# A vision-transformer layer on one core: the patch embedding of tiles 3 to 10 from fp16 high and low parts instead of fp32

## The reference

```
h = patches @ W.T + b                      # [32, 36, 768] x [768, 256]: the embedding
h = concat([cls_tok, h], axis=1)           # [32, 37, 256]
h = h + attention(layernorm(h))            # 4 heads, causal, with a linear memory read
h = h + moe(layernorm(h))                  # a shared FFN and the top 2 of 8 experts, hidden 1024
```

## Time and profile before

| | |
|---|---|
| median of 3 runs | 326.1 us (325.4 lowest, 1746.54 highest) |
| profiled execution | 325.89 us |
| its span | 324.0 us |
| granted TensorE clock | 0.996 |
| PE busy | 306.7 us, 95% |
| PEld busy | 259.6 us, 80% |
| DVE busy | 223.4 us, 69% |
| ACT busy | 184.5 us, 57% |
| POOL busy | 152.1 us, 47% |

### The profile page before, as it was taken

The page is one execution under the profiler, slowest core; times in us unless marked ns, Lnnn a source line. Parts: engine busy times, 40 slices in busy tenths (PEclk is TensorE's granted clock), DMA queues, the critical chain, the costliest instruction groups (busy, mean ns, idle before and its releaser), DMA issues.

```text
span 324.0 us, 9888 instructions
## 1 busy us (share of the span) xinstructions
PE 306.7 (95%) x3521; PEld 259.6 (80%) x3521; DVE 223.4 (69%) x502; ACT 184.5 (57%) x355; POOL 152.1 (47%) x208
## 2 busy tenths in 40 slices
PE   8789999999998999999999999999999999999990
PEld 6678788988777999999997777777787787777870
DVE  0637888888898989999886868755554546565530
ACT  1366768878896978476768878733232332323220
POOL 0577747777586322112622344656353544434131
PEclk9999999999999999999999999999999999999998
DMA  7775335322241117814798774243323242333121
GB/s 231 260 222 210 108 111 179 111 83 77 77 124 58 32 31 205 269 24 95 195 275 309 185 239 110 45 67 41 60 42 59 34 67 35 54 48 46 22 34 16
DMA packets 18642, 36.37 MB, mean 112 GB/s; under 512 B 3331, under 2 KB 10982, under 8 KB 18598
## 3 DMA queue, kind: packets, MB, share of 16 engines
q1 hardware_dynamic: 12166, 27.71, 26.2%
q0 software_dynamic: 6432, 8.03, 16.3%
HBM read 28.52 MB, written 7.21 MB: 110 GB/s over the span
## 4 chain that ended last, share of the span: by engine, by line
PE 76%; DVE 9%; DMA 4%; POOL 3%; issue 3%; ACT 2%; SPq 1%; POOLq 1%; DVEq 0%; ACTq 0%
PE bank L820 21%; PE bank L833 14%; PE bank L643 7%; PE bank L835 6%; PE bank L500 6%; PE bank L602 6%; DMA out_rows<-y,add_id 2%; PE bank L525 2%; PE bank L551 2%; DMA weights<-in_patches 2%; PE bank L591 2%; PE bank L565 1%; PE bank L555 1%; DVE weights L1309 1%; PE bank L453 1%
## 5 line engine op out<-in xcount | busy, mean ns | idle before, releaser
L820 PEld LDWEIGHTS bank<-x_t,weights 128*128 x1248 | 87.5, 98 | 25.5 <-issue 0.2
L820 PE MATMUL bank<-x_t,weights 128*128 128x128 f16 x1248 | 103.8, 219 | 0.0
L1002 ACT ACTIVATE act_out<-bank 128x512 f32<-128x512 f32 (+2 forms) x72 | 42.0, 585 | 86.1 <-PE bank L820 71.8
L1270 POOL DMA_INDIRECT out_rows<-y,add_id x26 | 43.0, 1653 | 69.6 <-DVE y L1626 48.1
L833 PE MATMUL bank<-weights,hid_hi 128*128 x192 | 73.3, 382 | 0.2
L1417 DVE SCALAR_TENSOR_TENSOR hid_lo<-act_out,hid_hi 128x512 f16<-128x512 f32 (+2 forms) x72 | 48.6, 680 | 12.5 <-ACT hid_hi L1013 11.0
L835 PE MATMUL bank<-weights,hid_lo 128*128 x192 | 52.3, 273 | 0.0
L1423 DVE SCALAR_TENSOR_TENSOR weights<-stage,weights 128x1024 f16<-128x1024 f32 x36 | 43.0, 1221 | 0.7 <-ACT weights L959 0.7
L959 ACT ACTIVATE weights<-stage 128x1024 f16<-128x1024 f32 x36 | 36.8, 1049 | 0.0
L1237 POOL DMA_INDIRECT slot_rows<-x_rows,gather_id x26 | 28.0, 1075 | 13.0 <-DMA out_rows<-y 5.2
L500 PE MATMUL bank<-weights 128*111 128x256 f32 x132 | 31.3, 386 | 1.6 <-DMA weights<-in_patches 1.1
(11 more groups left out here) (164 smaller groups left out, 522.8 us busy)
## 6 DMA issues: line engine op xcount, KB each, us to landing
stage<-in_w_ffn SPq DMA_DIRECT2D x36, 512.0 KB
weights<-in_patches SPq DMA_DIRECT2D x11, 333.0 KB, 3.3
x_rows<-rows SPq DMA_DIRECT2D x11, 111.0 KB
out_rows<-weights SPq DMA_DIRECT2D x10, 111.0 KB
out_rows<-y POOLq DMA_DIRECT2D x9, 119.0 KB, 5.3
weights<-in_w_embed SPq DMA_DIRECT2D x3, 256.0 KB, 4.2
stage<-in_w_qk SPq DMA_DIRECT2D x1, 512.0 KB, 6.9
slot_rows<-x_rows,gather_id POOLq DMA_INDIRECT x26, 4.1
```

The source lines that it names most:

```text
L820: mm = nc.tensor.matmul(o, weights[:, bass.ds(base + 2 * k * CHUNK + 2 * (col - col % D) + w * D + col % D, P)], x_t[:, b, (2 * x + k) * P ...
L1002: nc.scalar.activation(d_, s_, ACT.Silu, scale=1.0 / (X_SCALE * W_SCALE)).then_inc(hid_acted, 1)
L1270: nc.gpsimd.indirect_dma_start(out=out, out_offset=bass.IndirectOffsetOnAxis(ap=add_id[:, j:j + 1], axis=0), in_=y[:, y_place(j)], in_offs ...
```

## The change

- The embeddings of tiles 3 to 10 take three products of fp16 parts (low patches by high weights, high by low, high by high, in that order), so 18 fp16 matmuls for 6 fp32 ones. Tiles 0 to 2 stay as they are.
- The embedding's weights are split once, at the start: the high part is the first thing on ScalarE's queue (128x1024, then 128x512), the low part stands on VectorE between `embed_h(0)` and `embed_h(1)`.
- Each of tiles 3 to 10 has its patches (128x666) split. The high part is put at the end of ScalarE's step: tiles 3, 4, 5 and 6 in steps 0 to 3, and tiles 7 to 10 in steps 3 to 6 (two of them in step 3). The low part is put on VectorE behind `embed_h` in steps 0 to 2 (tiles 3 to 5), and from step 3 on between `split_lo` and `embed_h(s+2)` (tile `s+3`, to step 7).
- `embed_h` of these tiles scales and adds in one instruction, and the patches' buffer is free once the low part is written, not once the embedding is done.

```diff
+F16_FROM = 3
+P_SCALE = 16.0
+EMBED_PRODUCTS = ((1, 0), (0, 1), (0, 0))
...
             def load_patches(t):
-                if t >= PATCH_RING:
-                    sp.wait_ge(embed_ready, t - PATCH_RING + 1)
+                held = t - PATCH_RING
+                if held >= F16_FROM:
+                    sp.wait_ge(patch_lo, held - F16_FROM + 1)
+                elif held >= 0:
+                    sp.wait_ge(embed_ready, held + 1)
...
             def embed(t):
-                pe.wait_ge(patches_in[t % PATCH_RING], 16 * (t // PATCH_RING + 1))
+                if t < F16_FROM:
+                    pe.wait_ge(patches_in[t % PATCH_RING], 16 * (t // PATCH_RING + 1))
+                else:
+                    pe.wait_ge(patch_lo, t - F16_FROM + 1)
+                if t == F16_FROM:
+                    pe.wait_ge(we_lo, 2)
...
+                if t >= F16_FROM:
+                    for n, (x, w) in enumerate(EMBED_PRODUCTS):
+                        for k in range(PC):
+                            we = we_front[:, k, w] if k < 4 else we_back[:, k - 4, w]
+                            mm = nc.tensor.matmul(embed_bank(t), patch_pair[t % 2][:, x, k * T:(k + 1) * T], we,
+                                                  start=(n == 0 and k == 0), stop=(n == 2 and k == PC - 1))
+                    mm.then_inc(embed_ready, 1)
+                    return
...
+            def split_patches_hi(t):
+                act.wait_ge(patches_in[t % PATCH_RING], 16 * (t // PATCH_RING + 1))
+                if t >= F16_FROM + 2:
+                    act.wait_ge(embed_ready, t - 1)
+                nc.scalar.mul(patch_pair[t % 2][:, 0], s_patch[:, t % PATCH_RING].rearrange("p a b -> p (a b)"),
+                              P_SCALE).then_inc(patch_hi, 1)
...
                 if 0 <= s - 5:
                     copy_x2_t(s - 5)
+                if s <= F16_FROM:
+                    split_patches_hi(s + 3)
+                if F16_FROM <= s < NT - 4:
+                    split_patches_hi(s + 4)
...
+            def split_patches_lo(t):
+                dve.wait_ge(patch_hi, t - F16_FROM + 1)
+                nc.vector.scalar_tensor_tensor(
+                    out=patch_pair[t % 2][:, 1], in0=s_patch[:, t % PATCH_RING].rearrange("p a b -> p (a b)"),
+                    scalar=P_SCALE, in1=patch_pair[t % 2][:, 0], op0=ALU.mult,
+                    op1=ALU.subtract).then_inc(patch_lo, 1)
...
                 if s == 0:
                     embed_h(0)
+                    we_lo_of(0, we_front, s_we[:, 0:4])
+                    we_lo_of(1, we_back, s_we[:, 4:])
                     embed_h(1)
...
                 for c in chunks_at(s):
                     split_lo(c)
+                if F16_FROM <= s < NT - 3:
+                    split_patches_lo(s + 3)
                 if s + 2 < NT:
                     embed_h(s + 2)
+                if s < F16_FROM:
+                    split_patches_lo(s + 3)
```

More of the change, by code:

```diff
@@ L101, in build @@
         y = sb("y", [P, 3, D])
+        we_front = hid_hi.rearrange("p a b -> p (a b)").rearrange("p (k w d) -> p k w d", w=2, d=D)
+        we_back = hid_lo.rearrange("p a b -> p (a b)")[:, 0:2 * 2 * D].rearrange(
+            "p (k w d) -> p k w d", w=2, d=D)
+        patch_pair = [ap[:, 0:2 * PC * T].rearrange("p (w n) -> p w n", w=2) for ap in (
+            act_out.rearrange("p a b -> p (a b)").bitcast(F16),
+            slot_rows.rearrange("p a b -> p (a b)"))]
         space = weights[:, EARLY * EW:].bitcast(F32)
@@ L208, in build @@
         embed_ready = sem("embed_ready")
+        we_hi = sem("we_hi")
+        we_lo = sem("we_lo")
+        patch_hi = sem("patch_hi")
+        patch_lo = sem("patch_lo")
         h_ready = sem("h_ready")
@@ L1016, in shared_silu @@
                 silu_half(n, tokens_of(n), half_)
+            def split_patches_hi(t):
[4 more added lines that the diff above has]
+                              P_SCALE).then_inc(patch_hi, 1)
+            for part_ in range(EMBED_PARTS):
+                act.wait_ge(embed_in[part_], 16)
+                if part_ == 1:
+                    nc.scalar.mul(we_front[:, :, 0], s_we[:, 0:4], W_SCALE).then_inc(we_hi, 1)
+                if part_ == 2:
+                    nc.scalar.mul(we_back[:, :, 0], s_we[:, 4:], W_SCALE).then_inc(we_hi, 1)
             act.wait_ge(w_qk_in, 16)
@@ L1300, in embed_h @@
                     dve.wait_ge(rstd1, t - 1)
-                nc.vector.tensor_tensor(h[0:T, t % RING], embed_bank(t), s_eb[0:T],
-                                        ALU.add).then_inc(h_ready, 1)
+                if t < F16_FROM:
+                    nc.vector.tensor_tensor(h[0:T, t % RING], embed_bank(t), s_eb[0:T],
+                                            ALU.add).then_inc(h_ready, 1)
+                else:
+                    nc.vector.scalar_tensor_tensor(out=h[0:T, t % RING], in0=embed_bank(t),
+                                                   scalar=1.0 / (P_SCALE * W_SCALE), in1=s_eb[0:T],
+                                                   op0=ALU.mult, op1=ALU.add).then_inc(h_ready, 1)
                 dve.wait_ge(h_ready, t + 1)
@@ L1361, in proj_lo_of, with we_lo_of @@
                                                op0=ALU.mult, op1=ALU.subtract).then_inc(proj_lo, 1)
+            def we_lo_of(n, dst, src):
+                dve.wait_ge(we_hi, n + 1)
+                nc.vector.scalar_tensor_tensor(out=dst[:, :, 1], in0=src, scalar=W_SCALE, in1=dst[:, :, 0],
+                                               op0=ALU.mult, op1=ALU.subtract).then_inc(we_lo, 1)
+            def split_patches_lo(t):
[4 more added lines that the diff above has]
+                    op1=ALU.subtract).then_inc(patch_lo, 1)
             def xln_lo(t):
```

## The result

The changed kernel takes 332.93 us in the median of four executions (331.93 to 335.24), for 325.94 before: a ratio of 1.022 (95% interval 1.018 to 1.025). It is slower, by 7.0 us; 330.6 was forecast. Five more executions on another occasion gave 332.18 us and a ratio of 1.020 (1.018 to 1.022). The profiled execution took 331.93 us with a span of 329.6, 5.6 more than before.

A forecast was written before the change was run, and what follows sets the result against it. The prediction took PE as the bound, with VectorE 0.8 to 0.9 us below it. To 325.89 us it added 3.7 for the wait at tile 6 and 1.0 for GpSimd's loop: 330.6 us, range 327.6 to 333.4.

The forecast's parts named there:

- Which engines are near the bound: Steady steps of the front phase: PE full at 8.72 us, VectorE 0.8 to 0.9 us below it, idle only ahead of `embed_h`.
- The prices of the instructions: Per tile: eighteen fp16 matmuls 1.98 us for 2.77; low part 0.84 on VectorE, high part about 0.7 on ScalarE, `embed_h` sum 0.43.
- The weights' split at nothing: At the start: 1.9 us on VectorE and 1.7 on ScalarE, covered by waits, so counted as nothing; uncovered up to 1.9 us.
- The wait at tile 6: Step 3: VectorE stands 2.9 us for ScalarE's high part of tile 6; `residual(0)` comes 3.7 us late.
- GpSimd's loop: Steps 5 to 8: low parts block GpSimd up to 0.84 us, `residual` intervals become 9.3, 9.2, 9.2 us; 1.0 us in sum.
- The end: Step 8 gives back 0.3 us; the second phase, with PE 95% busy, takes up nothing of the delay.
- Rival 1: Steps 5 to 8: only the wait costs, GpSimd slips between two splits, steps of 8.9 us or less; 329.3 us, 15%.
- Rival 2: Steps 3 to 7: VectorE's five low parts each wait for a GpSimd operation, 5 x 0.5 us on top; 333 us, 9%.
- Rival 3: PE's idle before `mix_values(0)` and `scores(2)` halves its clock, costing 4 us more, part of it hidden by VectorE; 334 us, 6%.
- Rivals 4 and 5: 4: steps 9 to 12 give back 3 to 4 us, 327 us, 8%; 5: PE stays the bound, 320 us, 2%.
- The 1.5 us at tile 5: Steps 2 and 3: tile 5's low part waits for ScalarE's high part, so all after it on VectorE is 1.5 us late.

## Why the prediction was right, point by point

The direction, the mechanism and the range held (332.93 in 327.6 to 333.4). The point was 2.3 us short, and the measured time lies 0.5 us below the upper end of the range. The terms:

- **Which engines are near the bound** (VectorE 0.8 to 0.9 us below TensorE): right. The idle place ahead of `embed_h` vanished, and by the ratios the fp16 matmuls are worth 0.8 to 1.5 us, not 6.3.
- **The prices of the instructions**: right. The low part takes 0.85 us (0.84 forecast), the high part 0.76 (0.7), the sum in `embed_h` 0.41 to 0.43 as forecast, and the eighteen matmuls start in sixes 0.66 us apart, which makes the 1.98 us forecast.
- **The weights' split at nothing**: not quite. Its cover on VectorE and ScalarE was there, but GpSimd's chain beside it was blocked, by the same rule that I used later: L1201 took 1.11 us for 0.24, and `xln_lo(1)` came at 18.85 for 18.10. The shorter embedding of tile 3 only made up for that (`embed_h(3)` at 21.71 for 21.63), and `max_score(0)` was 0.83 us late for the 0.45 forecast. `max_score(1)` was at 33.55 for the 33.3 forecast, 31.81 before.
- **The wait at tile 6**: right in place and releaser, 3.35 us for 2.9. The delay at `residual(0)` was 4.20 for 3.7; this term of the sum was 0.5 too small.
- **GpSimd's loop**: right. 9.26, 9.39, 9.37 and 8.63 us for 9.3, 9.2, 9.2 and some 8.6. Blocking took 0.76 of the 0.84 us. The sum to tile 4 was 1.63 for 1.0, since the third interval before was 8.71 and not like the second, 8.96, which I had taken for it (0.25), and since the loop itself was taken too short for these steps: without the low parts it closes in 8.62 us there, and 8.62 and 0.77 are 9.39 for the 9.2 forecast.
- **The end**: 0.23 us came back behind tile 4. Outside the span lay 2.3 us for 1.9. With 0.5, 0.6, 0.4 and less 0.2 the profiled execution is at 331.9; the median of four is 1.0 above it. That last part was not in the sum.
- **Rival 1** (GpSimd slips through) is out by L1221 and L1223. **Rival 2** (VectorE is blocked) holds in part: L1365 at 0.98 for 0.39 in one kernel, the chunk's split at 1.80 for 1.21 in others, with a low part of 1.01 for 0.84 behind it in one of them; never for all five low parts. **Rival 3** (the clock): the half clock came, about where it was forecast, behind a gap of 2.23 us. In the changed kernel it was hidden, as TensorE still stood 0.79 us for VectorE ahead of `turn_attn(0)`; with VectorE's wait at tile 6 gone VectorE stood 1.52 us at `scores(2)`, and 0.32 us once the gap was filled: 1.2 us, for 4 less a part forecast, and 0.54 at `residual(0)`. What puts the median 1.0 above the profile is open: the clock is a candidate by the longest execution's mean of 0.981, but filling the gaps did not lower the median. **Rivals 4 and 5** are out: the delay was the same at the last tile, and without VectorE's instructions the gain was 1.6 us.

What I did not see is how much hangs on the early wait. The 1.5 us at tile 5 were one term among others. With the wait at tile 6 gone, moving tile 5's low part brought twice that: most of it already at `max_score(1)`, and the rest behind TensorE's gap, which grows or shrinks with it.

## What to carry to other kernels

Where two engines stand 10% apart, taking 0.8 us from the first and giving 0.85 to the second moves the bound; price what the change adds on the second engine first, and only then what it takes away. In queues written by hand, put each producer a step ahead of its consumer, or other work between them, for every tile, the first of the ramp too: the places of two instructions of the ramp and four of the steps made three quarters of this loss. And an instruction with two SBUF inputs on VectorE had a second price here, up to 0.77 us each time on GpSimd's chain; put it where GpSimd waits anyway.

## What was not expected of the hardware

- GpSimd and VectorE block each other in either direction: 2.31 us for 1.54 on GpSimd, 0.98 for 0.39 and 1.80 for 1.21 on VectorE. An early lead of 0.55 us was lost to one such meeting, in which the recorded starts of the two lie 0.02 us apart.
- TensorE's granted clock fell to half behind gaps of 2.0 to 2.5 us in some executions and not in others: behind 2.23 us in both profiles of the changed kernel but not in that with the low parts ahead of `residual`, behind 2.01 us in the run with all gaps filled but not in that with one. In one execution it fell behind gaps of 0.40 and 0.91 us close together; six of the same kernel's other seven executions ran at 0.991 to 0.995 in the mean and were 2.3 to 2.9 us shorter. Behind the one gap of 1.01 us it stayed full.
- Matmuls of ones kept the clock up in the place where they stood. With all gaps filled half clock came behind the next gap, and no gain in the median shows.
